# The three guard DMAs of each global-attention guard issued by ACT instead of SP

## The reference, cut to what matters

```
x = x + conv_attention(x)                    # 8 images, 1024 positions, q and k 16 wide
t = tokens(x)
t = t + L1(layernorm(t))                     # L1: global attention (8 heads, 16 wide) and
                                             # local attention (4 heads, window 5), fused, then an FFN
t = t + mixture_of_experts(layernorm(t))     # 8 experts, capacity 1280 rows each
# global attention, for each image and head:
scores = q @ k.T / sqrt(16); attn = softmax(scores); o = attn @ v
```

## Time and profile before

| | us |
|---|---|
| median of 3 runs | 2126.31 (2124.22 to 2127.44) |
| the profiled execution, its own time | 2125.43 |
| its span in the profile | 2123.7 |
| granted clock of PE, mean | 0.872 |
| PE busy | 1633.8 (77%) |
| DVE busy | 1344.7 (63%) |
| ACT busy | 1034.9 (49%) |
| POOL busy | 721.1 (34%) |

### The profile page before, as it was taken

How to read it: one execution, slowest core, us unless ns; L and a number is a source line. 1 busy time by engine, 2 the same in 40 slices (tenths; PEclk the granted TensorE clock), 3 DMA queues, 4 the chain that set the end, 5 groups by cost and what they waited for, 6 DMA issues and landing times.

```text
span 2123.7 us, 30139 instructions
## 1 busy us (share of the span) xinstructions
PE 1633.8 (77%) x8264; PEld 779.9 (37%) x8264; DVE 1344.7 (63%) x2698; ACT 1034.9 (49%) x1978; POOL 721.1 (34%) x1113
## 2 busy tenths in 40 slices
PE   4737979797798869796979697889779774187773
PEld 2412323433343335333433343343223222166552
DVE  3247878697679757884878587869669411134441
ACT  1311646575456636673667366647546652133331
POOL 3100310253225322433244224424424522436663
PEclk7766999899989989997999799989889986598995
DMA  5160340533234142504240434042441100033336
GB/s 171 43 104 8 132 105 1 122 128 52 42 121 121 31 95 74 127 18 99 105 98 16 94 120 84 21 105 79 86 83 68 48 16 0 17 79 58 59 51 170
DMA packets 125957, 162.04 MB, mean 76 GB/s; under 512 B 19117, under 2 KB 86450, under 8 KB 125799
## 3 DMA queue, kind: packets, MB, share of 16 engines
q1 hardware_dynamic: 109926, 148.61, 27.3%
q0 software_dynamic: 13568, 7.31, 2.5%
q10 hardware_dynamic: 2304, 4.20, 0.5%
HBM read 103.36 MB, written 58.52 MB: 76 GB/s over the span
## 4 chain that ended last, share of the span: by engine, by line
PE 31%; issue 20%; POOL 16%; DMA 11%; DVE 9%; ACT 6%; SPq 4%; another core or an unknown queue 1%; POOLq 0%; ACTq 0%; DVEq 0%
PE bank L1193 6%; PE bank L1236 5%; PE bank L1267 5%; DMA ql_tok<-ql_d 5%; PE bank L1255 5%; POOL t_d L1104 4%; PE bank L1114 3%; ACT prob L1500 3%; DMA k_stack<-parts_d 2%; DVE gmax L1700 2%; POOL rstd L1022 2%; SPq L893 2%; POOL lprod L1048 2%; POOL lprod L1055 2%; PE bank L1185 2%
## 5 line engine op out<-in xcount | busy, mean ns | idle before, releaser
L1700 DVE TENSOR_REDUCE gmax<-bank 128x1 f32<-128x512 f32 x1024 | 663.9, 680 | 203.3 <-PE bank L1236 193.8
L1500 ACT ACTIVATE prob<-bank 128x512 f32<-128x512 f32 x1024 | 573.2, 595 | 426.1 <-PE bank L1255 380.7
L1236 PE MATMUL bank<-k_stack,q_stack 96*128 96x512 bf16 x1024 | 421.0, 414 | 143.6 <-DMA k_stack<-parts_d 102.8
L1255 PE MATMUL bank<-q_stack,k_stack 99*128 99x512 bf16 x1024 | 403.4, 402 | 59.7 <-ACT prob L1500 48.6
L1267 PE MATMUL bank<-prob,v_tok 128*32 128x512 f32 x2048 | 278.2, 616 | 0.0
L1236 PEld LDWEIGHTS bank<-k_stack,q_stack 96*128 96x128 bf16 x1024 | 104.6, 102 | 431.0 <-DVE gmax L1700 221.6
L1013 POOL TENSOR_TENSOR mv<-stats 128x4 f32<-128x4 f32 x64 | 13.1, 205 | 619.8 <-DVE stats L1672 618.0
L1255 PEld LDWEIGHTS bank<-q_stack,k_stack 99*128 99x128 bf16 x1024 | 101.9, 101 | 251.0 <-ACT prob L1500 170.2
L1048 POOL TENSOR_TENSOR lprod<-ql_tok,kv_win 128x640 f32<-128x640 f32 x64 | 111.5, 1762 | 184.4 <-DMA ql_tok<-ql_d 173.4
L1104 POOL DMA_INDIRECT t_d<-v_tok,token_e x80 | 132.1, 1651 | 106.4 <-DVE v_tok L1898 76.6
L1055 POOL TENSOR_TENSOR lprod<-ls,kv_win 128x640 f32<-128x640 f32 x64 | 80.6, 1281 | 171.9 <-DVE ls L1755 171.9
(11 more groups left out here) (210 smaller groups left out, 2396.8 us busy)
## 6 DMA issues: line engine op xcount, KB each, us to landing
kv_win<-kv_d SPq DMA_DIRECT2D x32, 1280.0 KB, 5.6
parts_d<-parts SPq DMA_DIRECT2D x16, 768.0 KB, 3.6
q_stack<-parts_d SPq DMA_DIRECT2D x96, 128.0 KB, 6.8
k_stack<-parts_d SPq DMA_DIRECT2D x96, 128.0 KB, 7.2
kv_d<-lqkv SPq DMA_DIRECT2D x64, 128.0 KB, 1.7
rows_d<-rows SPq DMA_DIRECT2D x10, 528.0 KB
cprob<-rows_d SPq DMA_DIRECT2D x8, 660.0 KB, 4.6
x_cm<-in_x_dram SPq DMA_DIRECT2D x8, 512.0 KB, 9.3
```

The lines of the kernel that those rows point to most:

```text
L1236: mm(max_ps[max_bank(n)][:, :], q_stack[quad][0:KROWS, h, i * P:(i + 1) * P], k_stack[quad][0:KROWS, h, j * HN:(j + 1) * HN], start=True, ...
L1255: mm(score_ps[n % 2][:, :], k_stack[quad][0:KM, h, j * P:(j + 1) * P], q_stack[quad][0:KM, h, half * HN:(half + 1) * HN], start=True, stop ...
L1500: nc.scalar.activation(prob[:, g % 2, h, :], score_ps[n % 2][:, :], ACT.Exp).then_inc(exp_made, 1)
L1700: v.tensor_reduce(gmax[:, h, i, j:j + 1], max_ps[max_bank(n)][:, :], AX.X, ALU.max)\
```

## The change

`guard_rows` moves from SP's functions to ACT's, unchanged but for the engine, and its entry in `PARTS` goes from SP at 0.3 us to ACT at 1.3 us. The DVE copy, the semaphores, the three transfers and their destinations are the same.

```diff
-    "guard_rows": [("dve", 0.13, 0.2), ("sp", 0.3, 2.5)],
+    "guard_rows": [("dve", 0.13, 0.2), ("act", 1.3, 2.5)],
...
-            def guard_rows(b, quad):
-                after(sp, max_free, b * 2 * (TILES + 1) + (quad + 1) * (TILES + 1))
-                for s in range(3):
-                    dst = q_stack[quad][KROWS + s:KROWS + s + 1, :, :].rearrange("a h (t p) -> a (h t) p", p=P)
-                    sp.dma_start(dst, gneg_rows[s * QH * NT:(s + 1) * QH * NT, :]).then_inc(guard_in[quad], 16)
...
+            def guard_rows(b, quad):
+                after(act, max_free, b * 2 * (TILES + 1) + (quad + 1) * (TILES + 1))
+                for s in range(3):
+                    dst = q_stack[quad][KROWS + s:KROWS + s + 1, :, :].rearrange("a h (t p) -> a (h t) p", p=P)
+                    act.dma_start(dst, gneg_rows[s * QH * NT:(s + 1) * QH * NT, :]).then_inc(guard_in[quad], 16)
```

More of the change, by code:

```diff
@@ L920, in _ @@
                           conv_guard=conv_guard, local_qkv=local_qkv, global_stacks=global_stacks,
-                          guard_rows=guard_rows,
                           local_dot=local_dot, store_t2=store_t2))
@@ L1548, in _ @@
                            x_tokens=x_tokens, conv_qk=conv_qk, conv_guard=conv_guard, conv_exp=conv_exp,
-                           a_channels=a_channels, global_qk=global_qk, score_tile=score_tile, o_copy=o_copy,
+                           guard_rows=guard_rows, a_channels=a_channels, global_qk=global_qk, score_tile=score_tile, o_copy=o_copy,
                            local_max=local_max, o_channels=o_channels, fuse1=fuse1, x1_channels=x1_channels, ffn1=ffn1,
```

## The result

| | before | after |
|---|---|---|
| median | 2125.26 us (4 runs, 2122.38 to 2127.44) | 2154.39 us (4 runs, 2148.36 to 2154.88) |
| ratio of the runs, 95% interval | | 1.0135 (1.0119 to 1.0152) |
| span of the profiled execution | 2123.7 | 2152.9 |
| mean granted clock of PE | 0.872 | 0.860 |

The forecast was 2126.1, range 2115 to 2136. The time is 18 us above the range.

The account below looks back on a forecast made before the run. Waits, not a full engine, were taken to bound the kernel, chiefly PE's for the stacks; -4.2 + 2.0 + 0.9 + 1.1 = -0.2 us against the profiled 2125.43 gave a median of 2126.1, range 2115 to 2136.

Parts of the forecast that it names:

- (f): Planner's order in the loop body: some maxima move ahead a place; 3.4 us over five passes either way, 0 in sum.
- a pass whose length changes by over 2 us for any cause that lies away from the two guards: Any pass: one of the signs listed beforehand that would show the forecast wrong; size over 2 us.
- (a): Middle of five loop passes, SP's side: first stack DMA goes out 0.84 us earlier each, a gain of 4.2 us.
- (b): Middle of the loop passes, ACT's side: work behind the guard shifts by 1.8 us, hidden by PE's stall; cost 0.
- (c): End of loop passes: ACT branches later, returning in 7.4 to 10.7 us; 0.5 us each, 2.0 for four; SP's earlier loads 0.
- (d): End of the pass of b = 0: guard ahead of tile 60's exp on ACT delays the last score product; 0.9 us.
- (e): Guard of b = 7: the guard holds ACT's `o_copy`, with the tail behind it; 1.0 us, ends 0 and 1.8.
- The first guard: Guard of b = 0 at the start: ACT is about done with `norm_t`; cost 0, at most some tenths.
- A place one earlier: Rival, mid-pass: guard ahead of tile 61's exp delays the last score product by 1.8 us; 2134.8 us, chance 0.13.
- ACT's late return: Rival, loop's end: ACT comes back 1.8 us late four times, 7.2 us instead of 2.0; 2131.3 us, chance 0.14.
- that transfers bound the landing: Rival, mid-pass: stacks land when they did, so no gain there; 2130.3 us, chance inside the forecast's 0.40.

Follow-up runs that it names:

- order_only: Kernel before, SP still issuing the guard DMAs, with every engine in the order that the changed cost entry gave the changed kernel; ratio 1.0145.
- body_only: Kernel before, SP issuing all guards, with the changed kernel's order in the loop body (b = 1 to 5) alone; ratio 1.0111.
- act_cost03: Changed kernel, ACT issuing, with the planner's cost of the guard's issue at 0.3 instead of 1.3; ratio 1.0137.
- quad1_act: Kernel before, its order held, with only quad 1's guards (middle of the passes, and b = 7) moved to ACT; ratio 0.9997.
- late_branch: Kernel before, SP issuing all guards, but ACT also waits for quad 0's guard copy at its body's end and so branches later; ratio 1.0000.
- quad0_hold: quad0_act with SP's first load of the next pass held until quad 0's guard rows have landed; ratio 1.0037.
- quad0_act: Kernel before, its order held, with only quad 0's guards (the loop's end, and b = 0) moved to ACT; ratio 1.0056.
- late_act: late_branch with four spare activations on ACT behind its wait for quad 0's guard, meant to delay its branch further; ratio 1.0037.

## Why the prediction was wrong, step by step

- **(f) failed, and it decides.** It priced the reordering at one 680 ns maximum per pass in either direction, 3.4 us at most, and at 0 in the sum. order_only measures 1.45%, some 30 us, and body_only 1.1% for the loop body alone. The error was to count close choices and price them by the one instruction that swaps. The entry changed PE's order in 117 blocks of the loop body (the count that the expectation of act_cost03 gives), and what an order costs lies in when the instruction comes that releases a wait. The last score product of quad 0 came 8.6 us after the start of quad 1's guard instead of 3.3, and the stacks, and PE behind them, 4.5 us later in each of five passes. Part of that is POOL beside the guard's chain on DVE (25.7 us of longer chains in the whole kernel), but act_cost03 has the late product without it. Why the planner's small change puts it there was not followed. The prediction's own sign had been "a pass whose length changes by over 2 us for any cause that lies away from the two guards". The passes did change by over 2 us, but at a guard: from the first score product of quad 0 to the start of quad 1's guard, the passes of b = 2 to 5 took 89.0 to 89.6 us before and 87.9 to 88.4 after (the first pass 84.9 and 88.0), and from first to last score product, with the guard inside, 88.2 to 92.9 before and 95.6 to 97.3 after. The prediction had read that place for (a), but priced a later product there only in a rival.
- **(a) was right in kind and nearly in size.** The first stack DMA follows the last score product by 0.42 us in quad1_act instead of 1.40, so it goes out 0.98 us earlier (0.84 forecast), and PE restarts, counted from that product, 0.6 us earlier there and 0.7 in the change (means of five passes), 2.9 to 3.7 us in all of the 4.2. In the change the product itself is 5.3 us late. As a gain in time it can't be told from nothing.
- **(b) held.** With before's order the issues on ACT cost nothing measurable in the middle (quad1_act).
- **(c) had the right return, 9.7 us, within its 7.4 to 10.7.** A later ACT branch as such was free (late_branch); a return behind PE's was not priced. What failed is its last sentence: SP's loads of the next pass "start that much sooner ... so 0". They go out beside the guard's rows, and PE waits 8.5 us more for those; what that costs isn't shown (quad0_hold). Its 1201.56 stands in no row; the rows have ACT's first activation at 1201.64, a difference of no weight.
- **(d) and (e)**: with the order held, (c), (d) and (e) gave +4.0. quad0_act, which has (c) and (d), measured 0.56%, 11.9 us (7.6 to 16.1) against 2.9. (e) lies in quad1_act and can't be seen; its heading says 1.0 and the sum takes 1.1.
- **The first guard** was set at 0 for ACT's side alone. In SP's order the loads of the local attention stood behind it (first at 211.5 us before, 185.9 after). With it gone POOL starts its products beside the guard's chain on DVE, which lasts 3.9 us instead of 1.3.
- **The rivals.** None had the time. "A place one earlier" came nearest in kind: a later last score product, so later stacks in five passes. But its trigger was ACT's issue ahead of an exp, while order_only has the late product with SP issuing, and its 1.8 us per pass for that product was 5.3. ACT's late return had its condition (a return of 9.5 to 10.1 us, 8.9 or more) and its price is not known; order_only, with ACT back ahead of PE, has the whole loss without it. The last, that transfers bound the landing, fails by (a). The rule cited there from the Trainium skill (DMA: Bandwidth & Descriptors), that a second issuing engine saves issue time only, agrees with the rows: from the first stack DMA to PE's product on the stacks pass 15.0 us in the kernel before and in the change.

## What to carry to other kernels

When an order is computed from a table of costs, a changed entry is a second edit: hold the order and change only the engine, or price the reordering as a draw whose spread is measured (here 0.3 to 1.9% slower in six of six). To see what an order costs, find the wait that each pass ends on, here PE's for the stacks, and follow when the instruction comes that releases it. When a DMA leaves a queue, look at what stood behind it there, since that now starts sooner, beside DVE or beside the transfer itself. And where PE stands some microseconds for data, idle products there were worth 1.2%, more than anything that the moved issue could have given; in a pause of 3 us for the guard they were worth nothing.

## What the runs showed of the hardware

- A DVE cast or subtraction of 0.18 or 0.19 us on 128x32 takes 1.12 to 1.48 us beside POOL's elementwise products of 128x640 or 128x512, and the reduction of 0.22 us does not.
- DMA issues on ACT took 0.61 us each (median), 0.59 on SP, and ACT's activations started between them (1112.75 between 1112.60 and 1113.24).
- ACT's sequencer took its branch at 1193.5 in late_act, while four activations ran from 1193.38 to 1194.29.
- From the first stack DMA to PE's first product on the stacks (12 DMAs of 128 KB) pass 14.6 to 15.4 us (means of five passes) in each of the eleven traces of the table, on five chips.
- One kernel differs by 1.5% between chips (2091.7 and 2123.8 us).
